# A graph network's second aggregation in fp32r passes, with the slice attention regrouped and the expert matrices loaded in parts

## What is computed

```python
agg = jax.ops.segment_sum(x[src], dst, num_segments=N)      # graph layer (GIN)
h = (1.0 + eps) * x + agg
h = jax.nn.relu(batch_norm(h @ W1 + b1, g1, be1))
h = jax.nn.relu(batch_norm(h @ W2 + b2, g2, be2))
# slice attention beside it, on the same x
q, k, v = x_mid @ Wq, x_mid @ Wk, x_mid @ Wv                # x_mid = x @ W_in + b_in, by heads
q, k = softmax(q, axis=-1), softmax(k, axis=-2)
# then 32 experts that each take 39 tokens: silu(t @ W_up[e // 4] + b) @ W_down[e] + b
```

## Time and profile before

| | |
|---|---|
| median of 3 runs | 1709.99 us (1709.91 to 1711.13) |
| the profiled execution's own time | 1717.42 us |
| its span | 1715.6 us |
| PE busy | 1502.2 us (88%), 7001 matmul records |
| DVE, ACT, POOL busy | 673.9, 357.6, 446.1 us |
| mean granted TensorE clock | 0.934 of full speed |
| DMA | 173.27 MB, 101 GB/s over the span |

### The profile page before, as it was taken

The page is one execution under the profiler, slowest core; times in us unless marked ns, Lnnn a source line. Parts: engine busy times, 40 slices in busy tenths (PEclk is TensorE's granted clock), DMA queues, the critical chain, the costliest instruction groups (busy, mean ns, idle before and its releaser), DMA issues.

```text
span 1715.6 us, 18145 instructions
## 1 busy us (share of the span) xinstructions
PE 1502.2 (88%) x7001; PEld 982.0 (57%) x7001; DVE 673.9 (39%) x1251; ACT 357.6 (21%) x591; POOL 446.1 (26%) x431
## 2 busy tenths in 40 slices
PE   5999969999987399899999888998999719998984
PEld 3547645544566387677777445556876616554641
DVE  7321067785047424466665262503252460110100
ACT  2210003111010332444444111002152101100110
POOL 4100030006011210688888451002010022222112
PEclk9999989999998699899999999999999659999997
DMA  6000010005000120211110430002002925999992
GB/s 196 0 0 1 2 50 1 26 1 188 0 0 7 74 83 2 61 31 38 24 23 9 118 61 0 25 0 98 1 1 101 379 94 227 398 404 399 418 420 77
DMA packets 24056, 173.27 MB, mean 101 GB/s; under 512 B 4527, under 2 KB 5113, under 8 KB 17706
## 3 DMA queue, kind: packets, MB, share of 16 engines
q1 hardware_dynamic: 20074, 166.66, 26.3%
q0 software_dynamic: 3584, 5.12, 1.4%
q10 hardware_dynamic: 313, 0.35, 0.1%
HBM read 153.06 MB, written 16.49 MB: 99 GB/s over the span
## 4 chain that ended last, share of the span: by engine, by line
PE 75%; DMA 9%; DVE 8%; issue 3%; POOL 3%; ACT 2%; POOLq 0%; SPq 0%; ACTq 0%; DVEq 0%
PE psum L919 16%; PE psum L928 8%; PE psum L950 6%; PE psum L1371 6%; PE psum L1167 5%; DMA out_x<-arena,idx 4%; PE psum L942 4%; PE psum L1155 3%; DMA arena<-in_w_down 3%; PE psum L1353 3%; PE psum L1126 3%; PE psum L1156 2%; PE psum L1066 2%; PE psum L1075 2%; PE psum L1293 2%
## 5 line engine op out<-in xcount | busy, mean ns | idle before, releaser
L919 PE MATMUL psum<-arena 125*128 125x512 f32 (+3 forms) x768 | 273.9, 518 | 1.9 <-ACT arena L727 0.7
L919 PEld LDWEIGHTS psum<-arena 125*128 125x128 f32 (+1 forms) x768 | 146.3, 191 | 129.3 <-issue 128.1
L632 POOL TENSOR_TENSOR arena<-arena 125x420 f32<-125x420 f32 x192 | 178.5, 930 | 27.6 <-ACT arena L844 0.9
L1371 PE MATMUL psum<-arena 128*39 128x512 f32 (+1 forms) x704 | 157.6, 604 | 14.5 <-DMA arena<-in_w_down 11.5
L1650 DVE TENSOR_REDUCE neg_max<-psum 125x1 fp32r<-125x1250 f32 x80 | 116.8, 1459 | 113.3 <-PE psum L1126 113.3
L844 ACT ACTIVATE arena<-psum 125x420 f32<-125x420 f32 x240 | 108.0, 521 | 130.8 <-PE psum L1156 130.8
L1371 PEld LDWEIGHTS psum<-arena 128*39 128x39 f32 (+1 forms) x704 | 51.2, 117 | 114.9 <-issue 112.9
L950 PE MATMUL psum<-arena 128*125 128x512 f32 (+3 forms) x344 | 111.1, 485 | 6.1 <-issue 2.4
L1167 PE MATMUL psum<-arena 125*64 125x210 f32 x960 | 102.7, 349 | 0.0
L703 POOL DMA_INDIRECT out_x<-arena,idx x32 | 44.8, 1399 | 216.3 <-DMA out_x<-arena,idx 192.8
L1353 PEld LDWEIGHTS psum<-arena 128*128 128x128 f32 (+1 forms) x704 | 95.4, 190 | 5.9 <-issue 5.8
(11 more groups left out here) (316 smaller groups left out, 2135.5 us busy)
## 6 DMA issues: line engine op xcount, KB each, us to landing
arena<-in_w_down SPq DMA_DIRECT2D x32, 2816.0 KB, 23.0
arena<-in_w_up SPq DMA_DIRECT2D x32, 682.5 KB, 19.3
a_spill<-arena SPq DMA_DIRECT2D x1, 5468.8 KB
arena<-a_spill SPq DMA_DIRECT2D x1, 5468.8 KB
bc<-k_dram SPq DMA_DIRECT2D x16, 312.5 KB, 4.5
gw<-in_gw SPq DMA_DIRECT2D x2, 2048.0 KB, 10.8
arena<-in_wkqv SPq DMA_DIRECT2D x1, 3072.0 KB, 18.8
k_dram<-arena SPq DMA_DIRECT2D x1, 2500.0 KB, 7.3
```

Source lines behind the costliest of these rows:

```text
L632: pool.tensor_tensor(SUMS[rnd % 2], SUMS[rnd % 2], PT[s % P_RING], ALU.add).then_inc(sum_added, 1)
L919: ins = pe.matmul(o[0:w, lo:hi], lhs(c, m), rhs(c)[:, lo:hi], start=c == 0, stop=c == k - 1)
L1371: ins = pe.matmul(o[64 * j:64 * j + CAP, :], ACTT[g % 2][0:w, f, at:at + CAP], DN[e % 5][0:w, f], start=f == 0, stop=f == FT - 1)
```

## The change

1. Second aggregation: XN2 is split into fp32r parts (high on ACT, low on POOL, in place of XN2, behind a store of XN2 to HBM); ADJ is converted to fp32r by ACT. Each block then runs 2 x 10 fp32r passes over the tiles, and one more of 40 rows for "heavy" nodes, those with a count above 4096, whose counts fp32r might not hold. The diagonal goes away: DVE drains the block as XN2T * (1 + eps) + sum.
2. Heavy nodes: DVE takes the row maxima of ADJ beside the first aggregation, PE turns them and DVE picks up to eight (between blocks of `agg0`, written out for that), POOL gathers their rows of the spilled counts (now 1250 rows of 5000 bytes) and, in layer 1, of XN2.
3. Slice work: `slice_qv` becomes `slice_q` (64 columns for each matmul) ahead of the aggregation and `slice_v` (128) behind it; the key transposes go behind block 0 of the aggregation. `sw_out` is loaded behind `gw1`.
4. Down matrices: four transfers each (3, 3, 3 and 2 of 11 tiles), on two semaphores; PE waits for the first six tiles of a pair at tile 0 and for the rest at tile 6.
5. Loads that shared a purpose share a semaphore (`edges`, `mix_w`, `biases`, `sage`, `r2`, `router`), and small constants are made by POOL at the start.

```diff
             sp.wait_ge(win_free, WINDOWS)
-            store_rows(spilled, a_spill, part(3, 0, TILES * N, TOK))
+            store_rows(spilled, a_spill.rearrange("(t p) n -> p t n", p=TOK), ADJ)
...
-            store_rows(loads["adj"], part(6, 0, TILES * N, TOK), a_spill)
+            store_rows(loads["adj"], ADJ1, a_spill.rearrange("(t p) n -> p t n", p=TOK))
...
-            sp.wait_ge(rows_full, ROW["slice_qv"] + 20)
-            load("sw_out", SW_OUT, a["w_out"].rearrange("p (k n) -> p k n", k=C))
+            xn2_v = xn2_dram.rearrange("(t p) d -> p t d", p=TOK)
+            for g, (lo, hi) in enumerate(GROUPS):
+                sp.wait_ge(ln_out, LN_OUT["l1"] + hi)
+                if g:
+                    sp.wait_ge(xn2_stored, 32 * g)
+                store_rows(xn2_stored, xn2_v[:, lo:hi], XN2[:, lo:hi])
             sp.wait_ge(cols_full, COL["agg1"] + 4)
             load("gw1", GW1, a["gw1"].rearrange("p (k n) -> p k n", k=C))
+            sp.wait_ge(rows_full, ROW["slice_v"] + TILES)
+            load("sw_out", SW_OUT, a["w_out"].rearrange("p (k n) -> p k n", k=C))
...
-                load(f"dn{e % 5}", DN[e % 5], a["w_down"][e].rearrange("p (j h) -> p j h", j=FT))
+                down = a["w_down"][e].rearrange("p (j h) -> p j h", j=FT)
+                for half, lo, hi in DOWN_PARTS:
+                    load(f"{half}{e % 5}", DN[e % 5][:, lo:hi], down[:, lo:hi])
...
+            pool.wait_ge(rows_free, ROW["heavy_node"] + 1)
+            pool.wait_ge(spilled, 32)
+            pool.indirect_dma_start(
+                out=heavy_counts, out_offset=None, in_=a_spill,
+                in_offset=bass.IndirectOffsetOnAxis(ap=heavy_idx[:], axis=0)).then_inc(heavy_gathered, 16)
...
+            for g, (lo, hi) in enumerate(GROUPS):
+                for t in range(lo, hi):
+                    pool.wait_ge(ln_out, LN_OUT["l1"] + t + 1)
+                    done(pool.tensor_tensor(X[:, t], X[:, t], XN2[:, t], ALU.add))
+                pool.wait_ge(xn2_stored, 32 * (g + 1))
+                pool.wait_ge(rows_full, ROW["l1_t"] + C * (g + 1))
+                for t in range(lo, hi):
+                    pool.wait_ge(xn2_hi, t + 1)
+                    pool.tensor_tensor(XN2_PARTS[1][:, t], XN2[:, t], XN2_PARTS[0][:, t].bitcast(F32),
+                                       ALU.subtract).then_inc(xn2_lo, 1)
+            pool.indirect_dma_start(
+                out=heavy_x, out_offset=None, in_=xn2_dram,
+                in_offset=bass.IndirectOffsetOnAxis(ap=heavy_idx[:], axis=0)).then_inc(heavy_gathered, 16)
             pool.wait_ge(loads["b_out"], 16)
             for t in range(TILES):
...
+            for t in range(TILES):
+                act.wait_ge(ln_out, LN_OUT["l1"] + t + 1)
+                act.activation(XN2_PARTS[0][:, t], XN2[:, t], ACT.Copy).then_inc(xn2_hi, 1)
+            for m in range(4):
+                i = COL["x_mid"] + m
+                act.wait_ge(cols_full, i + 1)
+                act.activation(XMID[:, m], col_psum(i)[:, 0:N], ACT.Identity, bias=v("b_in", m)).then_inc(cols_free, 1)
+                if m == 0:
+                    act.wait_ge(loads["adj"], 32)
+                for t in range(4 * m, min(4 * m + 4, TILES)):
+                    act.activation(ADJ1_R[:, t], ADJ1[:, t], ACT.Copy).then_inc(adj_hi, 1)
+            act.wait_ge(heavy_gathered, 32)
+            act.activation(heavy_x_parts[:], heavy_x, ACT.Copy).then_inc(heavy_hi, 1)
...
-            pe.wait_ge(diag_ready, TILES)
-            col_stage("agg1", 4, lambda t, m: XN2[:, t, ch(m)], lambda t: ADJ1[:, t], TILES)
+            slice_rows("slice_q", 64, BDQV[:, 0:64])
+            pe.wait_ge(adj_hi, TILES)
+            pe.wait_ge(xn2_hi, TILES)
+            pe.wait_ge(xn2_lo, TILES)
+            for m in range(4):
+                o = open_col(COL["agg1"] + m)
+                for lo, hi in CHUNKS:
+                    for i, x_part in enumerate(XN2_PARTS):
+                        for t in range(TILES):
+                            pe.matmul(o[:, lo:hi], x_part[:, t, ch(m)], ADJ1_R[:, t, lo:hi],
+                                      start=i == 0 and t == 0, stop=False)
+                    if m == 0 and lo == 0:
+                        pe.wait_ge(heavy_lo, 2)
+                    ins = pe.matmul(o[:, lo:hi], heavy_x_parts[:, ch(m)], heavy_rest[:, lo:hi], start=False, stop=True)
+                ins.then_inc(cols_full, 1)
+                if m == 0:
+                    pe.wait_ge(kn_ready, 2)
...
+            slice_rows("slice_v", 128, BDQV[:, 64:192])
...
+            done(dve.tensor_reduce(row_max[:], ADJ, AX.X, ALU.max))
...
+            done(dve.tensor_tensor(heavy_counts, heavy_counts, heavy_hi_counts[:].bitcast(F32), ALU.subtract))
+            dve.tensor_scalar(heavy_rest[:], heavy_counts, heavy_mask[:], None, ALU.mult).then_inc(heavy_lo, 1)
```

More of the change, by code:

```diff
@@ L34 @@
 TILE_CODE = 256
+EXACT_COUNT = 4096
+HEAVY_ADD = 2048
+HEAVY_ROWS = 40
+HEAVY_PARTS = (slice(0, 8), slice(32, 40))
 WINDOWS_W1 = 12
@@ L358, in build @@
         sum_full, sum_inverted, att_ready = sem("sum_full"), sem("sum_inverted"), sem("att_ready")
-        diag_ready = sem("diag_ready")
+        heavy_found, heavy_gathered, heavy_hi, heavy_lo = [
+            sem("heavy_" + n) for n in ("found", "gathered", "hi", "lo")]
+        xn2_hi, xn2_lo, xn2_stored, adj_hi = [sem(n) for n in ("xn2_hi", "xn2_lo", "xn2_stored", "adj_hi")]
         x_hi, x_lo, ws_hi, ws_lo = [sem(n) for n in ("x_hi", "x_lo", "ws_hi", "ws_lo")]
@@ L546, in _ @@
             pool.memset(ones_dk[:], 1.0).then_inc(ones_dk_ready, 1)
+            done(pool.memset(heavy_mask[:], 0.0))
+            for own in HEAVY_PARTS:
+                done(pool.memset(heavy_mask[own], 1.0))
+            pool.iota(node_id[:], pattern=[[TOK, TILES]], base=0, channel_multiplier=1,
+                      allow_small_or_imprecise_dtypes=True).then_inc(const_ready, 1)
             def rstd(name, g):
@@ L1103, in _ @@
             ins.then_inc(rows_full, 1)
-            pe.wait_ge(loads["rw2"], 16)
+            pe.wait_ge(loads["r2"], 2 * 16)
             pe.wait_ge(relu_ready, 1)
@@ L1245, in _, with slice_rows @@
-            pe.wait_ge(diag_ready, TILES)
-            col_stage("agg1", 4, lambda t, m: XN2[:, t, ch(m)], lambda t: ADJ1[:, t], TILES)
+            def slice_rows(stage, w, weights):
+                for t in range(TILES):
+                    o = open_row(ROW[stage] + t)
+                    for c in range(C):
+                        ins = pe.matmul(o[0:TOK, w * c:w * c + w], XMID[:, c, tok(t)], weights, start=True, stop=True)
+                    ins.then_inc(rows_full, 1)
+            slice_rows("slice_q", 64, BDQV[:, 0:64])
@@ L1707, in _ @@
                 dve.tensor_reduce(small[:, m:m + 1], col_psum(n)[:, 0:N], AX.X, ALU.max, negate=True).then_inc(kmax_ready, 1)
+            for t in range(TILES):
+                o = filled(ROW["slice_q"] + t)
+                dve.tensor_copy(SQ[:, t], o[0:TOK, 0:M]).then_inc(rows_free, 1)
             for m in range(2):
@@ L1730, in _ @@
             dve.tensor_tensor(sq4, sq4, qm.unsqueeze(2).to_broadcast([TOK, 80, SLICE]), ALU.mult).then_inc(sq_out, 1)
+            for m in range(1, 4):
+                drain_agg(m)
+            for t in range(TILES):
+                o = filled(ROW["slice_v"] + t)
+                dve.tensor_copy(SV[:, t], o[0:TOK, :]).then_inc(rows_free, 1)
             n = ROW["slice_q_t"]
```

213 lines of the change are left out of this document (127 added, 86 removed).

## The result

| | before | after |
|---|---|---|
| first comparison, median of 4 runs each | 1710.56 us (1709.91 to 1719.31) | 1670.99 us (1668.56 to 1671.16) |
| ratio, 95% interval | | 0.9744 (0.9724 to 0.9765) |
| control (`a_again` below) | 1715.22 us, 9 runs | 1666.60 us, 5 runs |
| ratio, 95% interval | | 0.9722 (0.9699 to 0.9744) |
| profiled execution, span | 1717.42, 1715.6 us | 1668.56, 1666.7 us |

The forecast was 1659 us (1646 to 1680), faster. Profile against profile it was -50.8 us, and the spans differ by -48.9.

The account below looks back on a forecast made before the run. TensorE's issue-order work was taken to bound the kernel up to the expert stage, then the last down matrix's landing and slow scatters. Terms sum to -50.8 from 1717.4, giving 1666.6; less 7.4, 1659 us (1646 to 1680).

Parts of the forecast that it names:

- Rival A: Expert stage: scatters get no faster, their time being set by something other than load row length; -36.6, 1673 us, chance 0.22.
- Rival B: Slice region: a new wait, `heavy_lo` or the splits 5 to 10 us late, gives back gain; 1667 us, chance 0.10.
- The aggregation, -34.0: Second graph aggregation: fp32r passes in place of fp32 bring 83.95 us down to 50.0, saving 34.0.
- 84 sweeps: Second aggregation: four blocks of twenty fp32r sweeps and one heavy-node sweep, each priced at 0.595 us, 50.0 us in all.
- Rival C: Second aggregation: fp32r sweeps are no shorter with 125 rows and counts as moving operand; 176 us, chance 0.01.
- (a): Slice work: splitting `slice_qv` into `slice_q` and `slice_v` takes 19.6 us for 16.4, adding 3.2.
- (b): Key transposes moved behind aggregation block 0: PE no longer waits for the key softmax, saving 4.4 us.
- (c): From the aggregation's end to `gin1`, without `slice_v`: 15.1 us for 19.3, saving 4.2.
- First aggregation, +2.8: First graph aggregation: PE's added `heavy_row` and `heavy_node` records plus a handover cost 2.8 us, bounds 0 to +6.
- (d): Expert stage's end: PE starts a pair on its first six tiles, so PE ends at 1688.2, saving 3.4 us.
- rival D: Expert stage: transfers a quarter as long feed the DMA engines worse, making the kernel slower; 1735 us, chance 0.04.
- (e): Expert scatters: shorter down rows cut their period to 5.7 us, emptying the queue behind PE; -14.2 including (d).

Follow-up runs that it names:

- a_again: Changed kernel run once more as a control, only a counting-loop wait's register masked; 1666.60 us, ratio 0.9722 to the kernel before.
- a_fp32_order: Changed kernel with the second aggregation's main passes in fp32 on XN2's high part alone, order and heavy passes kept; 1708.97 us, ratio 0.9969.
- a_down1: Changed kernel with each down matrix as one transfer of 22528-byte rows and one wait, as before the change; 1679.07 us, ratio 0.9783.
- a_wait_all: Changed kernel, four down transfers kept, but PE waits for all eleven tiles of both matrices ahead of each pair; ratio 0.9757.
- a_down2: Changed kernel with two transfers for each down matrix (six and five tiles), split wait kept; 1663.78 us, ratio 0.9701.

## Why the prediction was right, and where its terms were off

The mechanism held: the terms sum to -50.8 us against the profile, -48.9 was measured, the fp32r passes and the empty queue behind PE are its two large terms, and `a_fp32_order` and `a_down1` take each of them back. Two things were luck. The small miss of the sum is made of larger ones that offset each other: +2.9 in the aggregation and +4.8 up to PE's end, against -1.5 in the slice work, -0.5 in the second stretch and -3.8 ahead of `slice_k`, where the clock varies by as much. And the measured 1671 lies above the forecast's own spread (1650 to 1670), inside the range only because that was widened to 1680 for rivals A and B, neither of which happened. Of the signs that were named, two failed: waits for `in_w_down` above 1 us stayed, and the scatters are 7.2 us apart during the loads and not 5 to 6.

- **The aggregation, -34.0.** Measured 83.95 to 52.8 (57.0 from start to end, less 4.2 of transposes), -31.1. The step that failed is "84 sweeps" of one price: the four of 40 rows cost 1.7 us each, with what they do to the others, 6.8 in all and not 2.4. The 80 of 125 rows were a little cheaper than said, 0.573 each without such passes (11.46 us for twenty) where 0.595 was taken; that hides 1.8 of the 4.4. Rival C did not happen.
- **(a), (b), (c): -5.4.** Measured -6.9. `slice_q` 9.1 for 9.3, transposes 4.2 for 4.9, end of aggregation to `gin1` 25.0 for 25.4. The fp32 experiment confirms it by another way: with the heavy passes' 6.8 us against it, the stretch is as long as before.
- **The waits beside the aggregation** were all hidden, `heavy_lo` by 1.5 us. Rival B did not happen.
- **First aggregation, +2.8.** Measured 475.24 - 388.18 = 87.1 for 84.2, with 2.3 of it in `heavy_row`: +2.8. In the time it is lost in the chance ahead of `slice_k`.
- **(d), PE's end, -3.4.** It came out at +1.4 and +1.0. The split wait is worth what was said (3.2 to 3.6, `a_wait_all`), but "the bytes and the full stream stay, so no more than that is had from the loads" overlooked that less can be had: four short transfers cost 4.2. It is rival D in small, which the prediction priced only at its breakdown. The waits for `in_w_down` stayed (4.72 at 1608.35).
- **(e), the scatters.** The period was to be 5.7 us and is 7.2. The law "six rows of load" is wrong at the short end (3.2 us extra for 1.4), while at 12288 and 10240 bytes a straight line between the two measured points holds (8.0 us for 7.9). The size did not matter, since the queue is empty at the end as soon as a group's four scatters fit in 35 us; with four transfers they take 29. The 5 us that the prediction added for the gathers are not to be added with such rows, as `a_down2` shows. So the last scatter follows PE's end by 6.1 us where 6.0 was said, -10.8 for -10.8. Rival A did not happen; `a_down1` puts the queue back.
- **The base, -7.4.** Terms and sum stood against the profile and were right there: 1666.6 forecast, 1668.6 measured. The subtraction that made it 1659 took a profile above its median for a fixed offset. Later medians of the kernel before were 1713 to 1715, and the changed kernel's profile lay below its median. The kernel before took from 1709.9 to 1722.7 us over the comparisons, so the 7.4 was chance, and 1659 was 8 to 12 us too low for it.

## What to carry to other kernels

Cut profiles at events and compare the stretches: in the first stretch two profiles of one kernel agreed within 0.1 us where its five timed runs spread over 5. Behind waits for a stream of loads that is 1 to 2 us, so take more than one profile there. When a large load is split to shorten what queues behind it, ask for the longest rows with which the queue just empties, since four and eleven cuts cost the stream here. In this kernel a single fp32r matmul between large ones was cheapest with their number of rows: zeros were cheaper than a change of shape.

## What the runs showed of the hardware that was not expected

- **Rows and the stream.** 407, 406, 402 and 383 GB/s with down rows from 22528 to 2048 bytes, in transfers over 128 partitions.
- **Partitions.** Transfers into 32 partitions with rows of 22528 bytes ran at 229 to 233 GB/s while the DMA engines showed a share of 0.99 to 1.01. The Trainium skill (SBUF — State Buffer, Door 1: The DMA port swizzle) says that DMA bandwidth goes by how many of the 16 ports the partitions reach, and by its table 32 neighbouring partitions reach 8 of them. The trace agrees: the rate is 0.57 of that with one transfer (231 for 407), and half the rate for the down matrices alone, the up matrices being as they were, would by an estimate from their bytes be 0.55.
- **Rows of the operands.** An fp32r matmul of 512 columns took 0.24 us among others of 125 rows, one of 40 rows between them 0.42, and ten matmuls between two such took 2.41 us for 2.32. Between fp32 matmuls the same 40-row pass cost a block 1.7 us as well (22.7 for 21.0). Why is not shown.
- **The granted clock** ahead of the first aggregation differed between executions of one kernel (0.98 or 1.00 in the first 100 us, 0.91 or 0.96 from 182 to 220), and the first aggregation began 3.2 us earlier in the one with the higher clock (385.0 for 388.2).
- **Gathers beside a scatter.** Four small gathers issued while a scatter is on its way added little with load rows of 12288 and 10240 bytes: the next scatters follow after 8.1 and 8.9 us in `a_down2`, where 8.0 is the usual. With rows of 22528 bytes they follow after 10.2 and 14.8 in the kernel before, where 9.5 is.
